# Cross-attention and a routed feed-forward layer: gate halves side by side, one normalisation for each value group, the bias added by a transfer, and the low halves of the probabilities on GpSimd

## The reference

```python
x = x + xattn(layernorm(x), ctx, ctx, Wq, bq, Wk, bk, Wv, bv, Wo, bo)   # 16 heads of 32, softmax
x = x + ffn(layernorm(x), gate_w, expert_w)

def ffn(x, gate_w, expert_w):                  # 8 experts
    chosen = argmax(einsum('bsh,eh->bse', x, gate_w), axis=-1)
    onehot = one_hot(chosen, 8)
    return x + einsum('bsef,bse->bsf', einsum('bsh,efh->bsef', x, expert_w), onehot)
```

## Time and profile before

| | |
|---|---|
| median of 3 runs | 1034.24 us (1033.22 to 1035.83) |
| the profiled execution, time | 1033.0 us |
| its span, first to last instruction | 1031.1 us |
| mean granted clock of TensorE | 0.947 of full speed |
| TensorE busy | 934.9 us, 91% of the span |
| VectorE busy | 783.3 us, 76% |
| ScalarE busy | 555.8 us, 54% |
| GpSimd busy | 546.4 us, 53% |
| DMA | 149.51 MB |

### The profile page before, as it was taken

How to read it: one execution, slowest core, us unless ns; L and a number is a source line. 1 busy time by engine, 2 the same in 40 slices (tenths; PEclk the granted TensorE clock), 3 DMA queues, 4 the chain that set the end, 5 groups by cost and what they waited for, 6 DMA issues and landing times. The chain is left out here.

```text
span 1031.1 us, 27389 instructions
## 1 busy us (share of the span) xinstructions
PE 934.9 (91%) x8834; PEld 567.6 (55%) x8835; DVE 783.3 (76%) x1802; ACT 555.8 (54%) x907; POOL 546.4 (53%) x559
## 2 busy tenths in 40 slices
PE   7475799999989999999999999999883999999996
PEld 3332466566556665566656656656562555555553
DVE  7743578999868899896899988988876565656563
ACT  4236866866748667676686676764833121212120
POOL 2431345555644546645555555454443577777774
PEclk9786899999989999998999999999987899999998
DMA  8957536455652565653645565346725355555550
GB/s 244 257 148 199 126 89 151 111 146 125 164 148 63 146 137 133 164 111 107 153 111 146 124 159 151 87 110 139 285 83 169 100 171 166 164 168 174 170 171 31
DMA packets 85686, 149.51 MB, mean 145 GB/s; under 512 B 22849, under 2 KB 24693, under 8 KB 85567
## 3 DMA queue, kind: packets, MB, share of 16 engines
q1 hardware_dynamic: 73359, 111.89, 44.0%
q0 software_dynamic: 11664, 36.05, 9.2%
q10 hardware_dynamic: 544, 0.02, 0.1%
HBM read 58.65 MB, written 40.50 MB: 96 GB/s over the span
## 5 line engine op out<-in xcount | busy, mean ns | idle before, releaser
L824 POOL TENSOR_TENSOR p_lo<-pf,p_hi 77x512 f16<-77x512 f32 x128 | 148.6, 1166 | 239.8 <-ACT p_hi L1168 239.7
L1167 ACT ACTIVATE pf<-scoresT,exp_scale 77x512 f32<-77x512 f32 x256 | 174.2, 680 | 83.5 <-PE scoresT L1002 73.0
L1474 PE MATMUL mo<-e_w,x2T_hi 128*128 x576 | 184.3, 382 | 0.7 <-DVE x2T_lo L1511 0.7
L1168 ACT ACTIVATE p_hi<-scoresT,exp_scale 77x512 f16<-77x512 f32 x256 | 174.3, 681 | 0.0
L1494 ACT ACTIVATE x2T_hi<-mt 128x512 f16<-128x512 f32 x72 | 43.0, 597 | 183.6 <-PE mt L1463 183.6
L1521 DVE SCALAR_TENSOR_TENSOR res<-mo,inv,row 128x512 f32<-128x512 f32 x72 | 54.1, 751 | 91.3 <-PE mo L1474 91.3
L1002 PE MATMUL scoresT<-q_st,k_now 97*77 97x512 f32 x256 | 105.9, 463 | 14.4 <-ACT p_hi L1168 11.2
L824 DVE TENSOR_TENSOR p_lo<-pf,p_hi 77x512 f16<-77x512 f32 x128 | 104.8, 834 | 18.3 <-ACT p_hi L1168 16.9
L1253 DVE TENSOR_REDUCE negmax<-work 128x4 f32<-128x308 f32 x256 | 112.7, 469 | 6.5 <-PE work L1050 6.4
L1474 PE MATMUL mo<-e_w,x2T_lo 128*128 x288 | 109.9, 382 | 0.0
L979 PE MATMUL work<-xnT_hi,wq_hi 128*128 128x512 f16 x256 | 101.0, 395 | 5.5 <-DVE xnT_lo L1231 5.5
(11 more groups left out here) (228 smaller groups left out, 2242.4 us busy)
## 6 DMA issues: line engine op xcount, KB each, us to landing
q_st<-q_hi SPq DMA_DIRECT2D x256, 128.0 KB, 2.4
row<-rows_by_expert SPq DMA_DIRECT2D x72, 257.5 KB, 2.9
xt<-in_x SPq DMA_DIRECT2D x16, 1024.0 KB, 7.8
q_st<-q_lo SPq DMA_DIRECT2D x128, 128.0 KB, 2.5
pay<-in_L_ffn_expert_w SPq DMA_DIRECT2D x8, 1024.0 KB, 6.9
er<-in_L_ffn_expert_w SPq DMA_DIRECT2D x7, 1024.0 KB, 15.0
k_next<-key_stacks SPq DMA_DIRECT2D x5, 462.0 KB, 9.2
key_stacks<-k_nat_hi SPq DMA_DIRECT2D x8, 154.0 KB, 3.0
```

What stands on the lines that cost most here:

```text
L824: return tt.tensor_tensor(pp[1][0:LK, g % 2, j, :], pf[:, j, :], pp[0][0:LK, g % 2, j, :], ALU.subtract)
L1167: nc.scalar.activation(pf[:, j, :], sbank[n % SB][0:LK, :], ACT.Exp, scale=exp_scale[0:LK, :])
L1168: nc.scalar.activation(pp[0][0:LK, g % 2, j, :], sbank[n % SB][0:LK, :], ACT.Exp, scale=exp_scale[0:LK, :]).then_inc(sem("exp_done"), 1)
L1474: ins = nc.tensor.matmul(obank2[u % 2][:, :], x2T[ia][:, u % 2, k, :], w, start=k == 0 and n == 0, stop=k == KT - 1 and n == 2)
```

## The change

Five edits, here cut to their core.

1. The gate weights' high and low halves lie side by side as 16 columns (`gate_h`, `wogate_h`). The high half of the rows is multiplied by all 16 at once, the low half by the first 8 only: 32 matmuls for a product. VectorE adds the two halves of the columns with a `tensor_reduce` before it goes on, into `gx` and into `lg`.
2. The two PSUM banks of the values become one tensor with 256 columns for each tile. PV runs its 48 matmuls after one wait and signals once, and V is one reciprocal and one multiply for all 4 tiles.
3. The output bias is added to a chunk of `xt` by one accumulating DMA that GpSimd issues, in place of four additions on GpSimd.
4. P_DVE is 0: the `p_lo` of all 16 heads are done by GpSimd.
5. The orders follow. The last chunks' orders (VECTOR_LAST) change in the same way, as do the counts of the semaphores.

```diff
-P_DVE = 2
+P_DVE = 0
...
 VECTOR = order("""
-    T0 T1 NM C0 T2 C1 K T3 O0 B0 P00 P01 C2 Q0 O1 M00 B1 L0 C3 M01 L1 P10 P11 L2 Q1 M02 GC M03 L3 M10 M11 H P20 LE P21
-    M12 V00 V01 O2 M13 B2 Q2 R V10 V11 M20 SL P30 Q3 V20 M21 M22 M23 V21 P31 O3 M30 B3 GX VE V30 M31 M32 M33 V31
+    T0 T1 NM C0 T2 C1 K T3 O0 B0 C2 Q0 O1 M00 B1 L0 C3 M01 L1 L2 Q1 M02 GC M03 L3 M10 M11 H LE M12 V0 O2 M13 B2 Q2 R
+    V1 M20 SL Q3 M21 M22 M23 V2 O3 M30 B3 GX VE M31 M32 M33 V3
 """)
...
 GPSIMD = order("""
-    A0 A1 A2 P02 P03 A3 P12 P13 F P22 P23 P32 P33 G D
+    A P00 P01 P02 P03 P10 P11 P12 P13 F P20 P21 P22 P23 P30 P31 P32 P33 G D
 """)
...
-    gt = [sa(f"gate_{s}", [P, KT, E], F16) for s in ("hi", "lo")]
-    wg = [sa(f"wogate_{s}", [P, KT, E], F16) for s in ("hi", "lo")]
+    gt = sa("gate_h", [P, KT, 2, E], F16)
+    wg = sa("wogate_h", [P, KT, 2, E], F16)
...
-        obank = [st.enter_context(nc.psum_tensor(f"pv{c}", [P, 512], F32)) for c in range(2)]
+        obank = st.enter_context(nc.psum_tensor("pv", [P, TPC, 256], F32))
...
-            def x_plus_bo(i, t):
-                if t == 0 and not i.is_(0):
-
-                    wait_alone(pool, "xn_ready", TPC * (i.n + 1))
-                nc.gpsimd.tensor_tensor(xt[i.slot][:, t, :], xt[i.slot][:, t, :], bo_rep[:], ALU.add)\
-                    .then_inc(sem("x_plus_bo"), 1)
+            def x_plus_bo(i):
+
+                wait_alone(pool, "xn_ready", TPC * (i.n + 1))
+                nc.gpsimd.dma_start(xt[i.slot][:], bo_rep[:].unsqueeze(1).to_broadcast([P, TPC, DM]), accum_op=ALU.add)\
+                    .then_inc(sem(f"x_plus_bo{i.slot % 2}"), 16)
...
-                for h in range(2):
-
-                    pe.wait_ge(sem("normalised"), 2 * G + h + 1)
-                    for t in (2 * h, 2 * h + 1):
...
-                    ins.then_inc(sem("values_ready"), 1)
+                pe.wait_ge(sem("normalised"), G + 1)
+                for t in range(TPC):
+                    for j in range(HG):
+                        for n, (ip, iv) in enumerate(HL):
+                            ins = nc.tensor.matmul(obank[:, t, j * VC:(j + 1) * VC],
+                                                   pp[ip][:, g % 2, j, t * P:(t + 1) * P], v_now[iv][:, g * HG + j, :],
+                                                   start=n == 0, stop=n == 2)
+                ins.then_inc(sem("values_ready"), 1)
...
                     for t in range(TPC):
+                        col = 2 * E * t
                         for k in range(KT):
-                            ins = product(ps[:, t * E:(t + 1) * E], [v[:, k, t * P:(t + 1) * P] for v in a],
-                                          [v[:, k, :] for v in w], k == 0, k == KT - 1)
+                            if k:
+                                nc.tensor.matmul(ps[:, col:col + E], a[1][:, k, t * P:(t + 1) * P], w[:, k, 0, :],
+                                                 start=False, stop=False)
+                            ins = nc.tensor.matmul(ps[:, col:col + 2 * E], a[0][:, k, t * P:(t + 1) * P], w[:, k, :, :],
+                                                   start=k == 0, stop=k == KT - 1)
...
-            def normalise(i, g, h):
...
+            def normalise(i, g):
+                dve.wait_ge(sem("values_ready"), KT * i.n + g + 1 + 2)
+                o = obank[:, :, 0:HG * VC].rearrange("p t (j k) -> p t j k", j=HG)
+                do(nc.vector.reciprocal(den[:], o[:, :, :, DK]))
+                nc.vector.tensor_tensor(cc[:, :, g * P:(g + 1) * P].rearrange("p t (j k) -> p t j k", j=HG),
+                                        o[:, :, :, 0:DK], den[:].unsqueeze(3).to_broadcast([P, TPC, HG, DK]), ALU.mult)\
                     .then_inc(sem("normalised"), 1)
+
+            def halves(ps):
+                return ps[:, 0:TPC * 2 * E].rearrange("p (t s e) -> p t e s", t=TPC, s=2)
...
-                    do(nc.vector.tensor_tensor(gx[:, n % 2], by_tile(ps), std[:, n % 2, :].unsqueeze(2)
+                    do(nc.vector.tensor_reduce(gx[:, n % 2], halves(ps), X, ALU.add))
+                    do(nc.vector.tensor_tensor(gx[:, n % 2], gx[:, n % 2], std[:, n % 2, :].unsqueeze(2)
...
-                    dve.wait_ge(sem("x_plus_bo"), TPC * m.n + t + 1)
+                    dve.wait_ge(sem(f"x_plus_bo{par}"), 16 * (m.b * (CPB // 2) + m.c // 2 + 1))
...
-                    return nc.vector.scalar_tensor_tensor(out=lg[:], in0=by_tile(ps), scalar=inv_gc[:], in1=gx[:, m.slot % 2],
+                    do(nc.vector.tensor_reduce(lg[:], halves(ps), X, ALU.add))
+                    return nc.vector.scalar_tensor_tensor(out=lg[:], in0=lg[:], scalar=inv_gc[:], in1=gx[:, m.slot % 2],
```

More of the change, by code:

```diff
@@ L99 @@
 VECTOR_LAST = order("""
-    NM C0 C1 C2 C3 O0 B0 P00 P01 O1 B1 O2 B2 P10 GC H O3 B3 VE P11 E00 E01 P20 R SL V00 V01 E02 E03 P21 E10 E11
-    V10 V11 P30 E12 E13 P31 E20 E21 V20 V21 E22 E23 V30 V31
+    NM C0 C1 C2 C3 O0 B0 O1 B1 O2 B2 GC H O3 B3 VE E00 E01 R SL V0 E02 E03 E10 E11 V1 E12 E13 E20 E21 V2 E22 E23 V3
 """)
@@ L271, in build @@
     negmax = sa("negmax", [P, TPC, H])
-    den = sa("den", [P, 2, 2, HG])
+    den = sa("den", [P, TPC, HG])
     bst2 = sa("bst2", [P, TPC, 6])
@@ L576, in _ @@
                     nc.scalar.activation(wgf[:].rearrange("p k e -> p (k e)"), ps[:, 0:KT * E], ACT.Copy)
-                    last = scaled(wg[0][:].rearrange("p k e -> p (k e)"), ps[:, 0:KT * E], S_WG)
+                    last = scaled(wg[:, :, 0, :], ps[:, 0:KT * E].rearrange("p (k e) -> p k e", k=KT), S_WG)
                 last.then_inc(sem("prep_act"), 1)
@@ L665, in gate_split @@
             def gate_split():
-                do(nc.vector.tensor_scalar(gt[0][:], gT[:], scl[:, S_G:S_G + 1], None, ALU.mult))
-                lo(gt[1][:], gT[:], scl[:, S_G:S_G + 1], gt[0][:])
+                do(nc.vector.tensor_scalar(gt[:, :, 0, :], gT[:], scl[:, S_G:S_G + 1], None, ALU.mult))
+                lo(gt[:, :, 1, :], gT[:], scl[:, S_G:S_G + 1], gt[:, :, 0, :])
                 nc.vector.tensor_scalar(bq_s[:], bvec[:, BQ, :], scl[:, S_WQ:S_WQ + 1], None, ALU.mult)
@@ L708, in _ @@
                 elif kind == "wg":
-                    last = lo(wg[1][:].rearrange("p k e -> p (k e)"), ps[:, 0:KT * E], scl[:, S_WG:S_WG + 1],
-                              wg[0][:].rearrange("p k e -> p (k e)"))
+                    last = lo(wg[:, :, 1, :], ps[:, 0:KT * E].rearrange("p (k e) -> p k e", k=KT),
+                              scl[:, S_WG:S_WG + 1], wg[:, :, 0, :])
                 elif kind == "bo":
@@ L1067, in banked @@
                     for t in range(TPC):
+                        col = 2 * E * t
                         for k in range(KT):
-                            ins = product(ps[:, t * E:(t + 1) * E], [v[:, k, t * P:(t + 1) * P] for v in a],
-                                          [v[:, k, :] for v in w], k == 0, k == KT - 1)
+                            if k:
[3 more added lines that the diff above has]
+                                                   start=k == 0, stop=k == KT - 1)
+                            if k == 0:
+                                nc.tensor.matmul(ps[:, col:col + E], a[1][:, k, t * P:(t + 1) * P], w[:, k, 0, :],
+                                                 start=False, stop=False)
                     return ins
@@ L1174, in _ @@
         def _(dve):
-            own = OwnCount(21)
+            own = OwnCount(19)
             def mark(ins):
@@ L1396, in iteration @@
                         own_parts[kind](i, *at)
-                        if (kind, *at) == ("V", KT - 1, 1) and i.slot == CPB - 1 and not i.is_(NCHUNK - 1):
+                        if (kind, *at) == ("V", KT - 1) and i.slot == CPB - 1 and not i.is_(NCHUNK - 1):
                             copy_v(i.plus(1).batch)
```

14 lines of the change are left out of this document (4 added, 10 removed).

## The result

The changed kernel took 1049.07 us (median of 4 runs, 1044.39 to 1050.48) against 1034.3 before (4 runs): a ratio of 1.0134, 95% interval 1.0118 to 1.015. Slower, and outside the range of 1025 to 1043. The profiled execution has a span of 1047.2 us, against 1031.1.

The account below looks back on a forecast made before the run. TensorE was taken as the bound, VectorE a close second; -0.04 us a pass over 14 passes (-0.6) plus -0.6 in the last two made -1.2, so 1033.0 us, range 1025 to 1043.

Parts of the forecast that it names:

- if the casts and the last `tensor_scalar` are held too ... between 0 and 0.35 I take 0.15: SL on VectorE, before `q_lo` and O3: GpSimd's subtractions hold its small steps, making O3 later by 0.15 us a pass.
- GC: "-0.1": Gate step before O2: shorter product, but multiply-add held by GpSimd; O2 wins 0 to 0.2 us, taken as 0.1.
- Casts were never seen beside GpSimd's work: Argument for the rival that nothing holds VectorE: 1029 us, or 1024 if GX's saving is won too; chance 0.26.
- The chain from O3 to O0: "-0.09": VectorE's chain between passes: one normalisation saves 0.31 us, GX's reduction costs 0.22, so minus 0.09 a pass.
- -0.04: Forecast net change of a full pass in us, from GC -0.1, chain -0.09 and SL +0.15.
- The first passes ... 0: Start of the kernel: first passes wait for ScalarE, weights and instructions, so the change costs or wins 0 there.
- Cost 0, covered by that slack: Bias by accumulating DMA: 5.5 us for the issue and 39 us for the transfer suffice, so no cost.
- GpSimd doesn't let VectorE in between two instructions: Rival: GC's multiply-add and SL wait through several GpSimd instructions, 3.1 us a pass, 1077 us (one place 1050 to 1060); chance 0.12.
- SL over 3 us long: Sign named in advance that would show the forecast wrong, in VectorE's step SL before `q_lo`.
- The DMA on GpSimd: Rival: the accumulating DMA holds GpSimd over 5.5 us; at 8 us, +2.5 us a pass, 1068 us; chance 0.05.
- the clock: Rival: TensorE idles more between O3 and O0, losing 0.03 of clock, 1.2 us a pass, 1050 us; chance 0.03.
- VectorE's relief: VectorE loses 128 `p_lo`, busy time down by over 88 us, yet it barely matters and the span stays nearly unchanged.

Follow-up runs that it names:

- after_again: The changed kernel as it is, measured a second time: 1041.37 us, ratio 1.0073 to the kernel before.
- sl_late: The changed kernel with SL moved behind V2 in VectorE's order: 1032.72 us, ratio 0.9999 to the kernel before.
- gate_norm: The kernel before with only the 16-column gate and the single normalisation: 1044.26 us, ratio 1.0104.
- only_bias: The kernel before with only the bias added by one accumulating transfer a chunk: 1036.62 us, ratio 1.0026.
- gate_norm_psum: The kernel before with 16-column gate and single normalisation, GC folding the halves in two steps that each read PSUM: 1030.01 us, ratio 0.9959.
- before_sl_late: The kernel before with only SL moved, behind V21: 1060.7 us, ratio 1.0241.
- undo_bias: The changed kernel with the bias again added by four GpSimd additions a chunk: 1032.91 us, ratio 0.9988.

## Why the prediction was wrong

*The step that failed: "if the casts and the last `tensor_scalar` are held too ... between 0 and 0.35 I take 0.15".* The mechanism was there and its size was not. I let both casts pass at one hand-over of GpSimd and the last step at the next. Of the sixteen times that SL runs, the two casts were parted in twelve, and in eleven of these the last step needed a third hand-over. In the second trace of the changed kernel (after_again) O3 comes 13.68 us behind O2, against 12.94 before: 0.74 us where I took 0.15, twice the upper bound of 0.35. sl_late takes it away.

*GC: "-0.1".* It gained more: O2 at 18.23 us against 18.58, so -0.35. I read the `negmax` as what O2 waits for, though it ended 0.2 us before O2; TensorE was the limit, and nearly all 0.41 us of the shorter product count. That I had the step held briefly was right for the changed kernel (0.29 us); that the same step can lose a whole subtraction by starting 0.03 us behind its start (gate_norm, 0.9 us a pass) I had only as a rival, and for another reason. "Casts were never seen beside GpSimd's work" overlooked one: a cast of a single element at 660.76 us took 0.14 beside a subtraction.

*The chain from O3 to O0: "-0.09".* Right: in the same pass 9.33 us from O3 to the next cast of the maxima, against 9.43. O0 starts 0.15 us behind `cT_lo`. The gate product measures 0.81 us (427.24 to 428.05), as said.

So a pass has -0.35 +0.74 -0.10 = +0.29 us, where I had -0.04, and the ordinary ones are 40.8 long against 40.5. Over 14 passes that is 4.1 us.

*The second step that failed: "The first passes ... 0", with "Cost 0, covered by that slack" of the bias by transfer.* The slack holds in ordinary passes, as only_bias shows. At the start it doesn't. With the transfer at the head of GpSimd's order the first exponential of the second pass stands 6.5 to 7.6 us behind the cast of the maxima in all six traces that have it there, and 4.9 in the nine without a transfer and in both with the transfer moved back: 1.6 us or more, once. The first cast of a maxima row comes at 87.2 to 90.7 us in those six (mean 88.8), and at 84.6 to 88.2 in nine without a transfer (mean 86.2); the expert loads of the same moment are the likely cause, but those times scatter too much by themselves to say how much.

*The rest.* 4.1 for the passes and 1.6 and about 3 for the start make 9; the second measurement is 7.4 us above the kernel before. Read off the casts of its trace, the start is the larger part: 6.3 of the 8.4 us between the spans are lost by the third cast (181.97 us for 175.66), 2.5 in the thirteen passes behind it, and 0.5 are gained after that. The first and third measurements are 14 to 15 us above the kernel before. In the first trace the thirteen passes lose 8.7 us in place of 2.5. What they have more is the late first exponential, which no row of the trace before announces and which stays unexplained.

*The rival "GpSimd doesn't let VectorE in between two instructions"* was to give 1050 to 1077 and be right if SL were held over 1.7 us. SL took 3.5 us, for 0.9, but this isn't that case: here VectorE got in at every hand-over, with one instruction. Its deciding mark was badly chosen, and so was "SL over 3 us long" as a sign of being wrong; even my own forecast had SL 3.05 us long. The DMA on GpSimd (1.45 us) and the clock (0.947) were no cause.

*What I said of VectorE's relief* was right in kind: its 66.6 us less bought nothing, since gate_norm_psum, which leaves the low halves as they were, is as fast as any kernel here within the intervals. They are fewer than the 88 that I named, since SL took back 34 us of them and the sums over the gate halves a little.

## What to carry to other kernels

Work moved to GpSimd is paid on VectorE in small instructions: a cast, a tensor_scalar or a multiply-add with all operands in SBUF can wait for a whole GpSimd tensor instruction (1.15 us here), one per hand-over, however little it does. Not every one does: see the list below. Count the small steps, place them where GpSimd idles and look at what then comes beside GpSimd instead (before_sl_late), or give them an operand in PSUM, as GC's step. With SL behind V2 and the bias by additions the same change is 0.45% faster than the kernel before (0.9955), where it was 0.7 to 1.4% slower as given. The gate and the normalisation alone, folded from PSUM, give the same 0.4%. And where two engines hold each other up like this, their phase decides: in undo_bias less than 0.01 us was worth 0.7 us a pass, and in gate_norm GC's step, issued 0.26 us later against GpSimd than in the changed kernel, cost 0.9, so that a part can lose alone what it wins among the others.

## What I had not expected of the hardware

- A multiply-add of 32 elements that reads SBUF alone took 1.17 us beside a GpSimd subtraction, and 0.25 us beside a like one with an operand in PSUM, both started within 0.1 us of its start.
- A tensor_scalar that reads SBUF isn't always held. In the third stage, before and after the change, 61 or 62 of its 72 on 128x512 elements start while a GpSimd addition that reads SBUF runs, and they take 0.54 to 0.56 us, as the ones without company do. What sets them apart from SL's and from the 4-element one at 732.59 was not tried.
- Two casts that follow each other 0.08 us apart when alone were separated by a hand-over in most passes: 0.60 and 1.21 us.
- Across additions that GpSimd runs without waiting between them VectorE isn't let in: 4.76 us for two casts, 4.43 of them in one that began 0.5 us before the three additions of 3.72 together, and 2.46 us for the subtraction of 390.46 before.
- An accumulating transfer of 1 MB from SBUF to SBUF took 1.45 us of GpSimd's time and landed after 10.9 us (median of 16).
- The same program took 1041 us in one measurement and 1049 in two, and no single time lies in both ranges.
